# A three-unit scan decoder on one core: projections of the last three sequences moved ahead and kept in DRAM, the experts' copies spread between loads

## The reference, cut to what matters

```
proj = rmsnorm(x, input_ln_w) @ w_in.T          # block A, 1024 channels
u, gate = split(proj)
u = silu(causal_conv1d(u, conv_w, conv_b))
t_r, Bm, Cm = split(u @ w_x.T)                  # each rmsnorm'd
dt = softplus(t_r @ w_dt.T + b_dt)
h = exp(dt * A) * h + dt * Bm * u               # 16 states, step by step over the tokens
y = (sum over states of h * Cm + u * D_skip) * silu(gate)
x = layernorm(x + x + y @ w_out.T + ffn(...))
```

## Time and profile before

| | us |
|---|---|
| median of three runs | 3246.27 |
| lowest, highest | 3241.14, 3251.11 |
| the profiled execution | 3242.18 |
| its span | 3240.4 |
| start of unit 0, unit 1, unit 2, unit 3 (first L1396 of each) | 52.9, 276.6, 443.3, 609.5 |
| start of units 6 and 9 | 1268.3, 1940.3 |
| last instruction of the scans (L1421 ends) | about 2608.9 |
| first L1596 of sequence 2's `xmix` | 2690.8 |

### The profile page before, as it was taken

The page is one execution under the profiler, slowest core; times in us unless marked ns, Lnnn a source line. Parts: engine busy times, 40 slices in busy tenths (PEclk is TensorE's granted clock), DMA queues, the critical chain, the costliest instruction groups (busy, mean ns, idle before and its releaser), DMA issues.

```text
span 3240.4 us, 20396 instructions
## 1 busy us (share of the span) xinstructions
PE 2410.5 (74%) x6316; PEld 1156.1 (36%) x6316; DVE 2482.0 (77%) x1928; ACT 1236.3 (38%) x1970; POOL 1044.1 (32%) x291
## 2 busy tenths in 40 slices
PE   5683121699888875899878866799787858979964
PEld 1241000244344433344434423344444424445532
DVE  5997989899798988897988988996999943121132
ACT  4433242443624535444435434434435413021222
POOL 0343545424345352323344462322353420000000
PEclk7875555799889986899889976899898878979986
DMA  2128000121216650222135630212146621216920
GB/s 89 39 101 230 0 7 0 32 67 49 75 67 190 212 156 7 77 67 67 51 110 188 216 111 13 78 62 63 46 132 199 202 71 70 73 42 207 294 79 13
DMA packets 151772, 312.07 MB, mean 96 GB/s; under 512 B 29872, under 2 KB 47280, under 8 KB 150064
## 3 DMA queue, kind: packets, MB, share of 16 engines
q1 hardware_dynamic: 130864, 261.41, 26.0%
q10 hardware_dynamic: 15680, 32.58, 2.9%
q0 software_dynamic: 5120, 16.78, 1.5%
HBM read 282.40 MB, written 43.78 MB: 101 GB/s over the span
## 4 chain that ended last, share of the span: by engine, by line
PE 35%; DVE 31%; issue 18%; ACT 9%; DMA 4%; POOL 3%; ACTq 0%; SPq 0%; DVEq 0%; POOLq 0%
DVE hb L1413 12%; PE ps L842 6%; PE ps L849 6%; DVE hb L1421 4%; DVE hb L1330 4%; PE ps L713 3%; PE ps L674 3%; DMA ring<-in_w_edn 2%; PE ps L885 2%; PE ps L980 2%; POOL ya L1690 2%; PE ps L776 2%; DVE sm L1274 1%; PE ps L815 1%; DVE hb L1396 1%
## 5 line engine op out<-in xcount | busy, mean ns | idle before, releaser
L1690 POOL TENSOR_TENSOR ya<-ya,hb 128x2048 f32<-128x2048 f32 x188 | 860.0, 4574 | 1371.1 <-DVE hb L1413 1296.5
L1413 DVE TENSOR_TENSOR_SCAN hb<-da,hb 128x2048 f32<-128x2048 f32 x192 | 865.3, 4507 | 7.3 <-ACT da L1020 6.0
L1020 ACT ACTIVATE da<-dl,pk 128x511 f32<-128x511 f32 x768 | 489.4, 710 | 487.0 <-DVE hb L1413 471.3
L1330 DVE TENSOR_TENSOR hb<-du,ps 128x2048 f32<-128x2048 f32 x192 | 435.9, 2270 | 33.1 <-POOL ya L1690 25.2
L1421 DVE TENSOR_TENSOR hb<-hb,ps 128x2048 f32<-128x2048 f32 x192 | 437.6, 2279 | 3.7 <-PE ps L790 2.9
L684 PE MATMUL ps<-bct,sel 64*128 64x512 f32 x192 | 109.6, 571 | 270.0 <-DVE hb L1330 263.4
L713 PE MATMUL ps<-V,ring 128*128 128x512 f32 x512 | 242.7, 627 | 25.7 <-DVE yg L1371 11.0
L674 PE MATMUL ps<-ring,hid 128*128 128x512 f32 x544 | 241.2, 599 | 7.6 <-DVE hid L1456 4.7
L870 PE MATMUL ps<-ring,hid 128*128 128x352 f32 x480 | 195.4, 491 | 20.3 <-ACT X L1199 20.1
L866 PE MATMUL ps<-ring,hid 128*128 128x352 f32 x480 | 199.5, 499 | 14.7 <-DMA ring<-egu 9.1
L790 PE MATMUL ps<-bct,sel 64*128 64x512 f32 x192 | 102.8, 535 | 135.6 <-DVE hb L1421 135.3
(11 more groups left out here) (242 smaller groups left out, 3341.1 us busy)
## 6 DMA issues: line engine op xcount, KB each, us to landing
ring<-egu SPq DMA_DIRECT2D x240, 352.0 KB, 3.7
ring<-in_w_edn SPq DMA_DIRECT2D x72, 512.0 KB, 5.2
ring<-in_w_fgu SPq DMA_DIRECT2D x44, 512.0 KB, 3.7
ring<-in_w_in SPq DMA_DIRECT2D x32, 512.0 KB, 3.6
hid<-xrows SPq DMA_DIRECT2D x60, 256.0 KB, 4.4
yrows<-X ACTq DMA_DIRECT2D x60, 256.0 KB, 4.7
ring<-in_w_egu SPq DMA_DIRECT2D x24, 512.0 KB, 3.3
ring<-in_w_edn SPq DMA_DIRECT2D x60, 192.0 KB, 4.3
```

The source lines that it names most:

```text
L1020: i = act.activation(dav(n % 2)[:, k, 1:], dl[:, k, 1:], ACT.Exp, scale=Aneg[:, (4 * (u % 3 - 1) if u % 3 else UC) + k, m:m + 1])
L1330: dve.tensor_tensor(hbv(m % NHB), du[:, :, :], wide(ps[:, 5, :], 4), ALU.mult).then_inc(s["dbu"], 1)
L1413: dve.tensor_tensor_scan(hb[:, h, :], da[:, b % 2, :], hb[:, h, :], 0.0, ALU.mult, ALU.add)\
L1690: pool.tensor_tensor(sums, ya[:, :, :], hbv(m % NHB), ALU.add).then_inc(s["acc"], 1)
```

## The change

Norm and all 16 column blocks of sequences 1, 2 and 3, with B, C and the low-rank part, are now computed in unit 1 and the start of unit 2. They use buffers that the chains need later only: `hid` for u, `X` and `T2` for the gate, `T1` and `R` for the small ones, and PSUM banks 0 to 3 in turn (four instead of two). `ACT` writes them to new DRAM tensors `su`, `sz`, `st`, `sr`, and each later sequence reads them back into `ucv`, `yg`, `tn` and `bct` when the sequence before has let go of these. The signals are split: `h_` now counts block A alone, and `c_` block B.

```diff
-        ready = (("c_bc", b, 0), "dve") if q % 3 == 0 else (("p_bs", b, 0), "dve")
+        ready = (("c_bc", b, 0), "dve") if q % 3 == 0 else (("t_load1", b, 0), "act", 5) if b else (("p_bs", b, 0), "dve")
...
-        put(20, ("hx_load", b, 0), "act", 0.1, (("t_sq", b - 1, 0), "pool") if b else None,
-            (("t_rs", b - 1, 0), "dve") if b else None)
+        put(20, ("hx_load", b, 0), "act", 0.1, (("p_mm", b - 1, 2 * UC - 1), "pe") if b else None)
...
+        if b:
+            u = 3 * b - 1
+            put(25, ("u_load", b, 0), "act", 0.1, (("skip", u, 0), "act"), (("dt_c", u, 0), "dve"), (("u_out", b, 1), "act", 9))
+            put(25, ("z_load", b, 0), "act", 0.1, (("mix", b - 1, 2 * KC - 1), "pe"), (("z_out", b, 1), "act", 9))
+            put(25, ("t_load1", b, 0), "act", 0.1, (("dt_mm", u, 3), "pe"), (("sb", NST * (u + 1) - 1, 0), "dve"),
+                (("t_out", b, 0), "act", 9))
...
+        su = nc.dram_tensor("su", [SEQS, 2, P, 4 * TOK], f32).ap()
+        sz = nc.dram_tensor("sz", [SEQS, 2, P, 4 * TOK], f32).ap()
+        st = nc.dram_tensor("st", [SEQS, P, TOK], f32).ap()
+        sr = nc.dram_tensor("sr", [SEQS, 2 * BC, TOK], f32).ap()
...
+        def ucb(b):
+            return hid[:, 0:UC, :] if b else ucv
+        def zb(b, g):
+            return yg[:, g, :] if b == 0 else X[:, g, :] if g < 4 else T2[:, g - 4, :]
...
+        def bank(b, n):
+            return n % 4 if b else 4 + 2 * (n % 2)
...
+                if t == "p_mm" and b and i % 2 == 0:
+                    n += [("relay", k, 0) for k in range(left, min(left + 3, len(copies)))]
+                    left = min(left + 3, len(copies))
...
-                    if b == 2:
-                        n += [("relay", e, 0) for e in range(EXP)]
...
+                        if b > 1 and n == 0:
+                            act.wait_ge(*of("h_tr", b - 1, 2))
+                        if b > 1 and n % 4 == 0:
+                            act.wait_ge(s[f"u_out{n // 4}"], 16 * (b - 1))
...
+                    elif t == "u_out":
+                        act.wait_ge(*of("h_u", b, 4 * n + 4))
+                        act.dma_start(su[b, n].rearrange("p (c t) -> p c t", t=TOK), ucb(b)[:, 4 * n:4 * n + 4, :])\
+                            .then_inc(s[f"u_out{n}"], 16)
...
+                    elif t == "u_load":
+                        act.wait_ge(s["skip"], 3 * b)
+                        act.wait_ge(s["delta"], 3 * b)
+                        for h in range(2):
+                            act.wait_ge(s[f"u_out{h}"], 16 * b)
+                            act.dma_start(ucv[:, 4 * h:4 * h + 4, :], su[b, h].rearrange("p (c t) -> p c t", t=TOK))\
+                                .then_inc(s["u_in"], 16)
...
                     elif t == "fin":
                         a = b % 3 - 1
                         dve.wait_ge(s["acc"], NST * (b + 1))
+                        if b > 2:
+                            dve.wait_ge(s["z_in"], 32 * (b // 3))
```

More of the change, by code:

```diff
@@ L108, in plan @@
         put(15, ("dt_b", q, 0), "pool", 4.6, (("dt_exp", q, 0), "act"))
-        put(50, ("dt_c", q, 0), "dve", 6.9, (("dt_b", q, 0), "act"), (("dt_b", q, 0), "pool", -2.2), (("sb", first - 1, 0), "dve") if q else None)
+        put(50, ("dt_c", q, 0), "dve", 6.9, (("dt_b", q, 0), "act"), (("dt_b", q, 0), "pool", -2.2), inner, (("sb", first - 1, 0), "dve") if q else None)
         put(40, ("dt_c", q, 0), "act", 2.8, (("dt_c", q, 0), "dve", -2.2))
@@ L157, in plan @@
         put(20, ("p_bb", b, 0), "pe", 3.6, at)
-        at = chain(20, ("p_bb", b, 1), [("pe", 3.6), ("act", 0.6)], (("p_bb", b, 0), "pe"), (("dt_mm", 3 * b, 3), "pe"))
+        at = chain(20, ("p_bb", b, 1), [("pe", 3.6), ("act", 0.6)], (("p_bb", b, 0), "pe"), (("dt_mm", 0, 3), "pe"))
         at = chain(20, ("p_bs", b, 0), [("pe", 0.9), ("act", 2.7), ("dve", 2.2)], at)
+        if b:
+            put(20, ("t_out", b, 0), "act", 0.1, at)
         for n in range(UC, 2 * UC):
-            put(35, ("p_mm", b, n), "pe", 3.6, at, (("p_gz", b, n - 2), "dve") if n >= UC + 2 else None,
-                (("p_mm", b, n - 1), "pe"))
+            free = ("p_gz", b, n - banks(b)) if n >= UC + banks(b) else ("p_ev", b, n - banks(b)) if b else ("p_bs", b, 0)
+            put(35, ("p_mm", b, n), "pe", 3.6, (free, "dve"), (("p_mm", b, n - 1), "pe"))
             chain(35, ("p_gz", b, n), [("act", 0.6), ("dve", 0.7)], (("p_mm", b, n), "pe"),
-                  (("mix", b - 1, 2 * KC - 1), "pe") if b else None,
+                  (("z_out", b - 1, (n - UC) // 4), "act", 9) if b > 1 else None,
                   (("p_gz", b, n - 1), "act") if n > UC else None)
+            if b and n % 4 == 3:
+                put(35, ("z_out", b, (n - UC) // 4), "act", 0.1, (("p_gz", b, n), "dve"))
+        if b:
+            u = 3 * b - 1
[3 more added lines that the diff above has]
+                (("t_out", b, 0), "act", 9))
     for k in range(FOLDS):
@@ L267, in plan @@
         put(60, ("t_load", b, 0), "act", 0.1, (("c_bc", b + 2, 0), "dve") if b + 2 < SEQS else
[L268 to L270 removed]
+            (("t_rs", b, 0), "dve"), at)
+        row = chain(60, ("att_qk", b, 0), [("pe", 1.9), ("act", 0.75)], (("t_load", b, 0), "act", 4))
         row = chain(60, ("att_qk", b, 1), [("pe", 1.9), ("act", 0.75)], row)
@@ L518, in pieces @@
             return out
+        copies = [(xrows, edn[0:NBLK * P, :])]
+        for e in range(EXP):
+            for cc, m, f, w in pieces(e):
+                for g in range(2):
+                    copies.append((egu[e, :, :, g * FE + f:g * FE + f + w].rearrange("k p m -> p k m"),
+                                   w_egu[cc].rearrange("p (g k m) -> p g k m", k=KC, m=P)[:, g, :, m:m + w]))
         def xb(j):
@@ L535, in loads @@
         def loads():
-            fold, n = 0, []
+            fold, left, n = 0, 0, []
             downs = {}
@@ L627, in _ @@
                             if b == 0:
-                                sp.wait_ge(s["relay"], 16 * (1 + 2 * sum(len(pieces(e)) for e in range(EXP))))
+                                sp.wait_ge(s["relay"], 16 * len(copies))
                         picked_e[j % 2] = sp.value_load(eidu[0:1, j:j + 1], min_val=0, max_val=EXP - 1)
@@ L726, in _ @@
                         pe.wait_ge(*of("h_bsq", b, 1))
-                        pe.matmul(ps[:, 6, :], ones, tn[:, :], start=True, stop=True).then_inc(s["h_tstat"], 1)
+                        pe.matmul(ps[:, 6, :], ones, tnb(b), start=True, stop=True).then_inc(s["h_tstat"], 1)
                     elif t == "p_bb":
@@ L1654, in _ @@
                         if b == 0:
-                            pool.wait_ge(s["relay"], 16 * (1 + 2 * sum(len(pieces(e)) for e in range(EXP))))
+                            pool.wait_ge(s["relay"], 16 * len(copies))
                         else:
```

336 lines of the change are left out of this document (196 added, 140 removed).

## The result

The changed kernel takes 3151.99 us (median of 4 runs, 3149.89 to 3153.88) against 3245.45 us before (4 runs, 3241.14 to 3251.11): a ratio of 0.972, 95% interval 0.970 to 0.974. I had said 3197 us, with a range of 3150 to 3245. The sign held. The median lies 2 us inside the lower edge of the range, outside my own band of 3180 to 3215 and in the one that I had given to the first rival, at 20%. The gain was forecast at 47 us and is 93, about twice that.

A forecast was written before the change was run, and what follows sets the result against it. DVE was taken as nearly full while units run, PE and latency as bounding the last chain. Terms -48 - 22 + 15 + 8 = -47 us gave 3197 us, range 3150 to 3245, own band 3180 to 3215.

The forecast's parts named there:

- the first rival: Feed-forward waits in the periods: without PE's projections there, 29.4 us of DVE idle go too, 3168 us; chance 20%.
- The frame: Up to sequence 2's first `xmix` addition DVE's instructions stay the same; time changes only by its idle time and durations.
- the 108 of my sum: DVE's projection work of three sequences, 108 us, moves from the periods into units 1 and 2, costing nothing by itself.
- the fourth rival: Moved norm, cast and silu wait for POOL's additions on a shared port: 27 us, 3224 us; chance 7%.
- The gap after the scans: Between scans' end and `xmix`: of 58.1 us idle DVE about 10 stay, a gain of 48 us.
- Waits that leave the periods: DVE's waits for the projections in the three periods go, a gain of 22 us.
- Unit 1: New waits where PE and DVE are level in unit 1: 5 us per sequence, a cost of 15 us.
- The handover to unit 2: `dt_mm` of unit 2 stands between pieces of `p_bc` and `p_bb`: mean to worst handover, a cost of 8 us.
- a low clock would set the pace: Rival in unit 1: PE slower than before on `p_mm` of sequences 1 to 3, 3250 to 3300 us; chance 12%.
- Spilling and reloading at 0: DRAM writes in unit 1 and reloads in the periods cost 0, upper bound 16 us.
- The copies: 57 expert copies, three at every second column block in unit 1; the ring holds five loads, some 30 us ahead.
- the three signs that would have made it wrong: Unit 3 starting beyond 765 us, over 30 us between scans' end and `xmix`, or later waits ending with a reload.

The follow-up runs named there:

- pool_small pair: POOL's additions of states cut from 2048 to 16 elements per partition: in the kernel before 3150.18 us (0.972), in the changed kernel 3084.05 us (0.951).
- late_comb: Changed kernel with one more dependency: the sum of the experts of sequence 2 waits for the scans' last `fin`; 3191.33 us (0.983).
- cut_before: Kernel before, order untouched, PE's and DVE's projection work of sequences 1 to 3 cut from 512 to 16 columns; 3200.82 us (0.988).
- two_banks: Changed kernel with two PSUM banks instead of four for the projections' products of sequences 1 to 3, order planned anew; 3154.17 us (0.972).
- one_load: Changed kernel with one ACT table load per unit instead of two, issued before ACT waits for the last product of `dt_mm`; 3136.89 us (0.968).
- spill_eighth: Changed kernel with the DRAM writes and reloads of u and z made on 16 of 128 partitions; 3156.63 us (0.974).

## Why the prediction was right, and where its sizes were off

*The frame.* Up to the first `xmix` addition DVE executes the same instructions, so that the time changes by its idle time: this held, and with it the direction. Its second half, "and by changes in duration", I then put at nothing without a reason. That is the step that failed: a term of 20.1 us stood at zero. I had weighed the collision with POOL only as a loss of moved work (the fourth rival, 7%), and the sum of all collisions came out as a gain.

The moved work itself has little part in it. The instructions of sequences 1 to 3 took 106.2 us before and take 104.3 in units 1 and 2, against the 108 of my sum. That 108 was too high, since I divided the group means of the earlier trace rows by four sequences alike. The cast's mean of 1376 ns holds one of 4257 ns, that of sequence 0, which does not move and takes 4255 ns after the change too. The three that move took 416 ns before and take 415 now. Before, from unit 3 to the scans' end:

```profile
L1383 DVE CAST bct<-bcf 32x512 fp32r<-32x512 f32 x3 | 1.2, 416 | 0.1
```

The other 18 us are instructions that were not moved with the projections and met POOL at other moments, in both directions: the attention's scaling went from 34.6 to 27.5 us, the scans from 865.3 to 858.5, while `fin` went from 18.3 to 22.7 and a scan over 8 elements (L1659) from 2.2 to 12.7 us (three of its four instances took about 4 us and ended 0.03 us behind an addition of POOL). The pool_small pair shows that the 20 us are POOL's. That they are a gain I had not worked out, and another order may turn the sign.

The Trainium skill, "SBUF — State Buffer", section "SBUF: two separate sides", has these two engines exclude one another for whole instructions. The trace agrees. One `fin` of the changed kernel, in DVE's and in POOL's order of time:

```profile
1121.19 6.67 DVE L1537 SCALAR_TENSOR_TENSOR yg<-ya,yg 128x2048 f32<-128x2048 f32 x1 [6.21 <-POOL ya L1802]
```

```profile
1121.18 4.53 POOL L1787 TENSOR_TENSOR dl<-dl,hb 128x2048 f32<-128x2048 f32 x1
```

Both start together, and `fin` takes 6.67 us where its like take 2.29: about 4.53 + 2.29, one behind the other.

*The gap after the scans*, -48 predicted, -51.2 measured, and late_comb returns 39.9 us of idle time for 39.9 us of span. Right in size and reason. I had 10 us left over; 6.9 were, all of them POOL's last addition.

*Waits that leave the periods*, -22 predicted. The projections' own waits did go, 19.6 us. But the periods gave 32.9 us. The step that was mis-sized is the rest of the order: the feed-forward gave 21.7 us, the scans' wait for `da` 6.0 (L1413), the segment attention's sum 5.1 (L1592) and the handovers 3.9, and new rows took 25.5 us; the rest is in small rows. That is the first rival, "more comes back", in three quarters of its size, but the new rows cancel more than it gave, and the net of 11 us beyond my 22 is a balance of many. Its reason, PE relieved of 77 us, has cut_before against it: with 32 of them taken from PE in place, and 21 from DVE, those waits grew from 29.4 to 41.1 us.

*Unit 1*, +15 predicted, 14.6 measured in the projections' own rows. The reason given (PE and DVE level, the norm's way and the input's load each time) fits the rows: PE waits there 19.7 us for ACT's squares and 14.1 for the norm, and ACT 10.4 us for the input's load. With half the banks, and its own order, two_banks takes no longer. That a low clock would set the pace did not come: the granted clock was 0.92 in the window of unit 1, against 0.50 before, near the upper of the two levels (2.4 GHz).

*The handover to unit 2*, +8 predicted, +2.2 measured: 6.8 us before, 9.0 after. It lies at the end of unit 1's window, whose +14.7 are 14.6 of the projections, 2.2 of this, 5.2 less before `fin`, and small gaps. All 11 handovers together fell from 90.5 to 88.9 us. I had moved it from the mean to the worst case because `dt_mm` stands among the pieces of `p_bc` and `p_bb`. ACT's own way is what holds it: where one_load shortens that by 28 us, the wait falls by 25.

*Spilling and reloading at 0*: right (spill_eighth).

*The copies.* I had three copies between loads cost about nothing, and no wait shows them. What I did not weigh is the other arrangement: kept in one piece they cost 42 us at their old place. So this half of the change keeps 42 of the 93 us; alone, in the kernel before, it was not run.

*What the profile was to show.* Unit 3 starts at 720.6, not 740: 3.7 us less of moved work than 108, 3.5 us off the scans of the two units (148.5 to 145.0), 8 us less of idle time than my 23, and some 4 us of overlap between neighbouring instructions, which a sum of groups counts twice. The scans end at 2591.7 (said 2630), `xmix` follows after 9.1 us (15), and 547.0 us remain (550). None of the three signs that would have made it wrong appeared.

The sum by the measured terms: -51.2 - 32.9 + 14.7 + 0 - 20.1 - 3.2 = -92.7 us, the difference of the spans but for rounding. Of the 46 us that I was short, 20 are the durations, 11 the periods, 8 unit 1 with its handover, 3 the gap, and 3 the start and tail. Part of this is luck: the periods and the durations are balances of gains and losses that I had not foreseen, and both came out on the same side.

## What to carry to other kernels

Where one engine is nearly full, count its idle time by stage and by what ends it, and ask of each wait whether the amount of foreign work or its position in a fixed order makes it: cutting the work in place helps to tell the two apart. Read single instructions before a mean is used as a price, since one collision can make most of it. Price the durations too, since an instruction that shares a resource with another engine changes its length when it is moved, in either direction. And when transfers are issued in one long piece, look at what load comes next in the same queue before moving anything to that place.
